# Turning the probabilities of a causal attention by VectorE block transposes and DMA in place of seven of ten TensorE transposes

## The chip, the cores and the metric

One Trainium2 chip, of which the kernel uses one core. The time is the device time of one launch in microseconds; of the kernel before it is 533.88 us, the median of 3 runs (533.76 to 533.94).

## The reference

The input is x of shape (2, 512, 256): two sequences ("halves") of 512 tokens. Four blocks are computed one after the other, each with its own parameter-free layer norm and a residual add.

```
x = x + attention0(layernorm(x))   # 3 heads, softmax over the query axis, mean over heads, fc
x = x + ffn(layernorm(x))          # ternary weights, silu(up) * gate, down
x = x + attention1(layernorm(x))   # 16 heads of 128, causal, biases
x = x + int8_linear(layernorm(x))  # per-token and per-row quantisation
```

The change is in attention1 alone. For each half b and head h it computes

```
q = x Wq + bq ; k = x Wk + bk ; v = x Wv + bv          # 512 x 128 each
scores = q k^T / sqrt(128), masked where key > query   # 512 x 512
attn   = softmax(scores over keys)
z      = attn v ;  out += z Wo ; out += bo
```

All of it is in float32. The kernel gets that accuracy from pairs of float32r operands: each operand is kept as a high part and a low part (operand minus high part), and a product is three matmuls, high*high, high*low and low*high (`split_mm`, L303 to L305).

## The kernel before, in words

Attention1 runs as 32 windows; window w is one half of the batch and one head. `PAIR_OF` and `HALF_OF` give the pair of heads and the half of each group of two windows; a pair of heads serves two groups, so its weights serve four windows. Tokens lie in four chunks of 128 (c = 0 to 3). Chunk c of the queries sees only key chunks 0 to c.

The work of one window, step by step:

- Q and K (`project_qk`, letters Q and K): two groups of six matmuls over 512 columns into PSUM; ScalarE writes the high part with the bias, VectorE the low part (`project_lo`, L1281). V (letter V, `project_v`): twelve matmuls over 256 columns, then a copy (L788) and a subtraction (L1278), letter W on ScalarE and VectorE.
- Scores (letter S, `scores`, L549 to L551): per chunk c three float32r matmuls over (c+1)*128 columns, but never under 256 (`n = max((c + 1) * P, 2 * P)`). VectorE adds the mask and takes the row maximum into `SM` (`max1`, L1291), ScalarE takes the exponential into `PR` and the row sum (`exp1`, L797), VectorE the reciprocals (`recip1`, letter R, L1298; R0 for chunks 0 to 2, R1 for chunk 3), GpSimd multiplies each chunk by them (`normalise`, L962 to L971, semaphore `p_norm`).
- The turn (letter T, `turn`, L559): to be the operand of the next product the probabilities must stand with the keys on the partitions. Chunk c takes c+1 TensorE transposes of 128 x 128 into PSUM bank 4 or 5, so a window has 1+2+3+4 = 10 of them. ScalarE copies the high part to `PT_hi` (`probs_hi`, L802), VectorE subtracts for `PT_lo` (`probs_lo`, L1302, semaphore `t_free`).
- z (letter A, or B when it belongs to the window before; `attend`): for each key chunk j three matmuls over the query columns from j*128 to 512, but never under 256. The zero blocks that the wider products read are set once. ScalarE and VectorE write `Z_hi` and `Z_lo` (L808, L1309).
- The output product (letter O, `project_out`): for both heads of a group together, 24 matmuls over 256 columns per half of the tokens, two such parts per group, then an add to X by VectorE (`add_out`, L1322).

Nothing is scheduled at run time. The order of the work on each engine is a string of letters with the chunk or part number, written by hand, one for even and one for odd windows, and the last windows have their own:

```python
EVEN_PE = steps("T0 T1 S0 O0 T2 T3 S1 Q0 S2 O1 K1 A0 S3 V2")
EVEN_DVE = steps("T0 T1 S0 W2 O0 T2 T3 S1 Q0 S2 O1 R0 K1 S3 A0 R1")
ODD_PE = steps("T0 T1 S0 Q0 T2 T3 S1 S2 K1 A0 S3 V2")
```

In window w, T and A are of window w, S and R of window w+1, Q, K and V of window w+2. Both output parts of a group fall in the even window, so even windows are longer than odd ones. Engines meet by semaphores only, and each engine works strictly in the order of its own string.

Four windows share one packed weight tile `stage` (1,027 KB, loaded by SyncE, L334). VectorE and GpSimd split it (`load_a`, `load_b`, `split_a`, `split_b`: L1214 to L1230 and L929, L935), and SyncE loads the next one when both have finished with it. In the steady windows SyncE has nothing else to do.

Of the kernel before, what the change touches and what calls it, by code (L numbers as in the profile page):

```python
# [15 lines left out]
F32 = mybir.dt.float32  # L16
# [7 lines left out]
P = 128  # L24
D = 256
# [11 lines left out]
FFN_STEPS = HALVES * ECH  # L37

# [15 lines left out]
def build(nc, x, wq0, wk0, wv0, fcT, fcb, wupT, wgateT, wdownT, pack1, bo1, qw, qb, out):  # L54
    ctx = ExitStack()
    with ctx:
# [74 lines left out]

        XQ1 = sb("XQ1", [P, CT, D])
# [16 lines left out]
        Z_hi = sb("Z_hi", [P, 2, SEQ], F32R)  # L149
        Z_lo = sb("Z_lo", [P, 2, SEQ], F32R)  # L150
# [8 lines left out]
        memf = ExitStack()  # L159
        SIL = sb("SIL", [P, 3, SEQ], F32, memf)  # L160
        HID = sb("HID", [P, 3, SEQ], F32, memf)
        HID_hi = sb("HID_hi", [P, 3, SEQ], F32R, memf)
        HID_lo = sb("HID_lo", [P, 3, SEQ], F32R, memf)
        memf.close()
# [42 lines left out]
        t_psum, pt_hi, t_free, pt_zero = sem("t_psum"), sem("pt_hi"), sem("t_free"), sem("pt_zero")  # L207
# [28 lines left out]
        LAST = {"pe": {WINDOWS - 2: steps("T0 T1 S0 S1 O0 S2 T2 T3 S3 O1"),  # L236
                       WINDOWS - 1: steps("T0 T1 B0 T2 A0 T3 O0 A1 O1 I0 I1")},
                "act": {WINDOWS - 2: steps("T0 T1 S0 S1 T2 S2 T3 W2 S3"),
                        WINDOWS - 1: steps("T0 T1 B0 T2 A0 T3 A1 X0 I0 I1")},
                "dve": {WINDOWS - 4: steps("T0 T1 S0 W2 O0 T2 T3 S1 L0 Q0 S2 O1 L1 R0 K1 S3 A0 R1 L2"),  # L240
                        WINDOWS - 3: steps("T0 T1 S0 W2 N0 Q0 T2 T3 S1 N1 S2 R0 K1 N2 S3 A0 R1 N3"),
                        WINDOWS - 2: steps("T0 T1 S0 S1 X0 S2 T2 R0 T3 W2 S3 O0 R1 X1 X2 O1"),
                        WINDOWS - 1: steps("T0 T1 B0 T2 A0 T3 X3 O0")}}

# [12 lines left out]

        def loads_k(w):

            return w % 2 == 1 and (w + 3) // 2 in FIRST_GROUP[1:]  # L260

        def window_work(engine, w):

            for kind, c in LAST[engine].get(w, ORDERS[engine][w % 2]):
                if w == 0 and kind == "O":
                    continue
                yield kind, c

# [43 lines left out]
        def _(sp):  # L312
# [33 lines left out]
        def _(pe):  # L346
# [192 lines left out]
            def scores(w, c):  # L539
# [6 lines left out]
                n = max((c + 1) * P, 2 * P)  # L546
# [7 lines left out]
            def turn(w, c):  # L554

                pe.wait_ge(p_norm, 4 * w + c + 1)
                pe.wait_ge(t_free, 4 * w + c + 1)
                for j in range(c + 1):
                    mm = pe.transpose(bank[4 + c % 2][:, j * P:(j + 1) * P], PR[:, c, j * P:(j + 1) * P], ident[:])  # L559
                mm.then_inc(t_psum, 1)  # L560

            def attend(w):

                g, h = divmod(w, 2)
                pe.wait_ge(t_free, 4 * w + 6)
# [3 lines left out]
                if w == 1:  # L569
                    pe.wait_ge(pt_zero, 1)  # L570
                for j in range(CT):
                    q0 = min(j * P, SEQ - 2 * P)
# [6 lines left out]
            def attend_half(r):  # L579
# [3 lines left out]
                pe.wait_ge(t_free, 4 * w + 4 + 2 * r)  # L583
                cols = slice(2 * r * P, 2 * (r + 1) * P)
                for j in range(2 * r + 2):
                    v = (slice(None), CT * (g % 2) + j, slice(h * DH, (h + 1) * DH))
                    mm = split_mm(pe, bank[2 + r][:, cols], V_hi[v], V_lo[v], PT_hi[w % 2][:, j, cols],
                                  PT_lo[w % 2][:, j, cols],
                                  j == 0, j == 2 * r + 1)
                mm.then_inc(z_psum, 1)  # L590

            def project_out(g, r):
# [9 lines left out]
                for i in range(2):  # L602
                    cols = slice((2 * r + i) * P, (2 * r + i + 1) * P)
                    for h in range(2):
                        mm = split_mm(pe, out_bank(g, r)[:, i * D:(i + 1) * D], Z_hi[:, h, cols], Z_lo[:, h, cols],
# [22 lines left out]
            def window(w):  # L628
                p = PAIR_OF[w // 2]
                for kind, c in window_work("pe", w):  # L630
# [13 lines left out]
                    elif kind == "O":  # L644
                        project_out(w // 2 - (w < WINDOWS - 1), c)
# [38 lines left out]
        def _(act):  # L684
# [115 lines left out]
            def probs_hi(w, c):  # L800
                act.wait_ge(t_psum, 4 * w + c + 1)
                act.copy(PT_hi[w % 2][:, 0:c + 1, c * P:(c + 1) * P],  # L802
                         bank[4 + c % 2][:, 0:(c + 1) * P].rearrange("p (j q) -> p j q", q=P)).then_inc(pt_hi, 1)

            def z_high(w):
                p, b, h = place(w)
                act.wait_ge(z_psum, w + 1)
                act.activation(Z_hi[:, h, :], bank[6][:], ACT.Identity, bias=bv[p % 2][:, h:h + 1],  # L808
                               scale=1.0).then_inc(z_hi, 1)

            def z_high_half(r):
                p, b, h = place(WINDOWS - 1)
                cols = slice(2 * r * P, 2 * (r + 1) * P)
                act.wait_ge(z_psum, WINDOWS + r)
                act.activation(Z_hi[:, h, cols], bank[2 + r][:, cols], ACT.Identity, bias=bv[p % 2][:, h:h + 1],
# [24 lines left out]

            def scale_tokens():
# [7 lines left out]
            def window(w):  # L849
                p = PAIR_OF[w // 2]  # L850
                for kind, c in window_work("act", w):
# [4 lines left out]
                    elif kind == "A" and w < WINDOWS - 1:  # L856
                        act.wait_ge(bv_ready, p + 1)
                        z_high(w)
                    elif kind == "A":
# [6 lines left out]
                    elif kind == "W":  # L866
                        if w == 0:
                            layernorm_hi(5)
                        project_hi(w + 1, c)
                    elif kind == "X":  # L870
# [14 lines left out]
        def _(pool):  # L885
# [99 lines left out]

            rstd(5)
# [17 lines left out]
        def _(dve):  # L1004
# [263 lines left out]
            dve.memset(PT_hi[0][:, CT - 1, 2 * P:3 * P].bitcast(F32), 0.0).then_inc(t_free, 1)  # L1268
            dve.memset(PT_lo[0][:, CT - 1, 2 * P:3 * P].bitcast(F32), 0.0).then_inc(t_free, 1)
# [30 lines left out]
            def probs_lo(w, c):  # L1300
                dve.wait_ge(pt_hi, 4 * w + c + 1)
# [89 lines left out]
            def window(w):  # L1391
                for kind, c in window_work("dve", w):
                    if kind == "T":
                        probs_lo(w, c)
                    elif kind == "S":
# [6 lines left out]
                    elif kind == "R":  # L1402
                        recip1(w + 1, c)
                    elif kind == "A" and w < WINDOWS - 1:
# [5 lines left out]
                    elif kind == "O":  # L1410
                        if w == 2 and c == 0:
                            dve.wait_ge(x_biased, 2 * TILES)
                        add_out(w // 2 - (w < WINDOWS - 1), c)
                    elif kind in "QK":
                        project_lo(w + 2, c)
                    elif kind == "W":
# [3 lines left out]
                        if loads_v(w):  # L1420
                            load_a(PAIR_OF[w // 2 + 1], 2)
# [9 lines left out]
                    if loads_v(w) and (kind, c) == (("O", 1) if w == WINDOWS - 8 else ("S", 1)):  # L1431
                        load_bv(PAIR_OF[w // 2 + 1])
# [68 lines left out]
```

## Time and profile before

| | |
|---|---|
| median of 3 runs | 533.88 us |
| the profiled execution | 534.24 us |
| its span | 532.4 us |
| TensorE busy | 514.5 us, 97% |
| VectorE busy | 385.2 us, 72% |
| ScalarE busy | 292.8 us, 55% |
| GpSimd busy | 191.9 us, 36% |
| chain that ended last | TensorE 86%, VectorE 7%, ScalarE 2%, DMA 2% |
| DMA | 17.52 MB in 8333 packets, most of it before 60 us |

The span is what the profiler saw between the first and the last instruction; 1.8 us of the execution lie outside it. Matmuls overlap, so a matmul's recorded time is longer than the distance to the next one; what a group of them costs is read from the distances between starts. In the tables of groups a name stands without its number, so `bank` is any PSUM bank and `PT_lo` either of the two.

### The profile page before, as it was taken

What the parts mean: (1) busy time and instruction counts of PE and PEld (TensorE: products, weight loads), DVE (VectorE), ACT (ScalarE), POOL (GpSimd) and SP (SyncE); (2) the same over time, 40 slices, a digit from 0 to 9 for tenths busy, and PEclk for the clock granted to TensorE, in tenths of its full rate; (3) what the DMA queues carried; (4) which work ended last, traced back from release to release, by engine and by line L of the source; (5) the groups of instructions that cost most, each with busy time, mean ns of one, the idle gap of its engine ahead of it and who ended that gap; (6) DMA issues with size and microseconds to landing.
All of it is one profiled execution on the core that took longest, in us unless ns stands there. A gap on an engine that the chain in (4) does not pass through costs nothing.

```text
span 532.4 us, 9326 instructions
## 1 busy us (share of the span) xinstructions
PE 514.5 (97%) x3302; PEld 464.4 (87%) x3302; DVE 385.2 (72%) x970; ACT 292.8 (55%) x688; POOL 191.9 (36%) x277
## 2 busy tenths in 40 slices
PE   8999999999999899999999999999999999999972
PEld 7888889898888789999999999999998999999861
DVE  2757876855555978768668668777777787667897
ACT  2446533564545565655656656566566565665552
POOL 2236142434656335214223223322512543222234
PEclk9999999999999999999999999999999999999995
DMA  9900000000000021000200200200200200000002
GB/s 281 356 6 1 1 0 1 2 1 1 2 0 1 0 81 46 36 1 1 80 1 1 81 2 1 79 2 2 80 0 2 80 2 0 2 1 0 2 2 79
DMA packets 8333, 17.52 MB, mean 33 GB/s; under 512 B 480, under 2 KB 6752, under 8 KB 7264
## 3 DMA queue, kind: packets, MB, share of 16 engines
q1 hardware_dynamic: 7200, 15.89, 8.7%
q10 hardware_dynamic: 1088, 1.05, 0.6%
q8 instruction: 27, 0.44, 0.3%
q14 instruction: 18, 0.15, 0.1%
HBM read 15.88 MB, written 1.05 MB: 32 GB/s over the span
## 4 chain that ended last, share of the span: by engine, by line
PE 86%; DVE 7%; ACT 2%; DMA 2%; issue 1%; POOL 1%; SPq 0%; DVEq 0%; ACTq 0%
PE bank L303 20%; PE bank L305 20%; PE bank L304 20%; PE bank L559 6%; PE bank L550 4%; PE bank L549 4%; PE bank L551 4%; PE bank L488 3%; PE bank L487 3%; DMA Wv_sb<-wv 2%; PE bank L498 1%; PE bank L500 1%; DVE XN L1021 1%; DVE SM L1291 1%; PE bank L354 1%
## 5 line engine op out<-in xcount | busy, mean ns | idle before, releaser
L797 ACT ACTIVATE PR<-SM,nmax 128x128 f32<-128x128 f32 (+3 forms) x128 | 71.9, 562 | 100.7 <-DVE nmax L1291 100.5
L1291 DVE CUSTOM_DVE_ANT_0 SM<-bank,causal 128x128 f32<-128x128 f32 (+3 forms) x128 | 60.7, 484 | 18.4 <-PE bank L551 18.3
L962 POOL TENSOR_TENSOR PR<-PR,rec 128x128 f32<-128x128 f32 x32 | 12.8, 400 | 140.2 <-DVE rec L1298 140.2
L1302 DVE TENSOR_TENSOR PT_lo<-bank,PT_hi 128x128 fp32r<-128x128 f32 (+3 forms) x128 | 59.3, 485 | 2.1 <-ACT PT_hi L802 0.3
L802 ACT CAST PT_hi<-bank 128x128 fp32r<-128x128 f32 (+3 forms) x128 | 50.0, 423 | 5.1 <-PE bank L559 4.3
L303 PE MATMUL bank<-XT_hi,W_hi 128*128 128x512 f32 x128 | 50.6, 395 | 0.2 <-DVE XT_lo L1029 0.2
L918 POOL TENSOR_TENSOR E_lo<-E,E_hi 128x512 fp32r<-128x512 f32 x24 | 31.0, 1297 | 54.6 <-ACT E_hi L721 47.6
L305 PE MATMUL bank<-XT_hi,W_lo 128*128 128x512 f32 x128 | 50.5, 395 | 0.0
L304 PE MATMUL bank<-XT_lo,W_hi 128*128 128x512 f32 x128 | 50.4, 394 | 0.0
L559 PE MATMUL bank<-ident,PR 128*128 128x128 f32 x320 | 46.2, 273 | 1.8 <-DVE PT_lo L1302 0.8
L549 PE MATMUL bank<-K_hi,Q_hi 128*128 128x256 f32 (+2 forms) x128 | 46.5, 364 | 0.0
L1281 DVE SCALAR_TENSOR_TENSOR Q_lo<-bank,bqk,Q_hi 128x512 fp32r<-128x512 f32 x32 | 24.0, 751 | 29.6 <-ACT Q_hi L791 29.6
L303 PE MATMUL bank<-PT_hi,V_hi 128*128 128x256 f32 (+2 forms) x130 | 41.9, 323 | 0.2 <-DVE V_lo L1278 0.2
L305 PE MATMUL bank<-PT_hi,V_lo 128*128 128x256 f32 (+2 forms) x130 | 41.9, 322 | 0.0
L304 PE MATMUL bank<-PT_lo,V_hi 128*128 128x256 f32 (+2 forms) x130 | 41.9, 322 | 0.0
L550 PE MATMUL bank<-K_lo,Q_hi 128*128 128x256 f32 (+2 forms) x128 | 41.5, 324 | 0.0
L559 PEld LDWEIGHTS bank<-ident,PR 128*128 128x128 f32 x320 | 37.0, 141 | 5.1 <-POOL PR L971 1.1
L551 PE MATMUL bank<-K_hi,Q_lo 128*128 128x256 f32 (+2 forms) x128 | 41.3, 322 | 0.0
L716 ACT ACTIVATE E<-bank,nmax 128x512 f32<-128x512 f32 x24 | 16.5, 687 | 41.8 <-DVE nmax L1094 41.7
L303 PE MATMUL bank<-WO_hi,Z_hi 128*128 128x256 f32 x128 | 35.8, 280 | 1.9 <-DVE Z_lo L1316 1.9
L969 POOL TENSOR_TENSOR PR<-PR,rec 128x128 f32<-128x128 f32 x32 | 13.6, 424 | 64.6 <-DVE rec L1298 64.6
L303 PE MATMUL bank<-W_hi,XT_hi 128*128 128x256 f32 x128 | 36.1, 282 | 0.0
(174 smaller groups left out, 1621.9 us busy)
## 6 DMA issues: line engine op xcount, KB each, us to landing
stage<-pack SPq DMA_DIRECT2D x8, 1027.0 KB, 4.9
X<-x SPq DMA_DIRECT2D x2, 512.0 KB, 8.8
wraw<-wupT SPq DMA_DIRECT2D x1, 1024.0 KB, 10.1
wraw<-wgateT SPq DMA_DIRECT2D x1, 1024.0 KB, 12.0
wraw<-wdownT SPq DMA_DIRECT2D x1, 1024.0 KB, 15.8
Wq_sb<-wq ACTq DMA_DIRECT2D x3, 256.0 KB, 5.3
Wk_sb<-wk SPq DMA_DIRECT2D x3, 256.0 KB, 4.7
Wv_sb<-wv SPq DMA_DIRECT2D x3, 256.0 KB, 8.4
```

Of the source, the lines that this page charges most:

```text
L303: pe.matmul(dst, a_hi, b_hi, start=first, stop=False, skip_group_check=share)
L304: pe.matmul(dst, a_hi, b_lo, start=False, stop=False, skip_group_check=share)
L305: return pe.matmul(dst, a_lo, b_hi, start=False, stop=last, skip_group_check=share)
L549: pe.matmul(dst[:, 0:n], Q_hi[:, slot, cols], K_hi[:, slot, 0:n], start=True, stop=False)
L550: pe.matmul(dst[:, 0:n], Q_hi[:, slot, cols], K_lo[:, slot, 0:n], start=False, stop=False)
L551: pe.matmul(dst[:, 0:n], Q_lo[:, slot, cols], K_hi[:, slot, 0:n], start=False, stop=True).then_inc(s_psum, 1)
L559: mm = pe.transpose(bank[4 + c % 2][:, j * P:(j + 1) * P], PR[:, c, j * P:(j + 1) * P], ident[:])
L797: act.activation(PR[:, c, 0:(c + 1) * P], SM[:, c % 2, 0:(c + 1) * P], ACT.Exp, bias=nmax1[:, c:c + 1], scale=-1.0, accum_out=sum1[:, c:c ...
L802: act.copy(PT_hi[w % 2][:, 0:c + 1, c * P:(c + 1) * P], bank[4 + c % 2][:, 0:(c + 1) * P].rearrange("p (j q) -> p j q", q=P)).then_inc(pt_ ...
L918: pool.tensor_tensor(E0_lo[:, m, :], E0[:, m, :], E0_hi[:, m, :], ALU.subtract).then_inc(e0_lo, 1)
L1291: dve.tensor_tensor_reduce(SM[:, c % 2, 0:n], bank[2 + c % 2][:, 0:n], causal[:, SEQ - n:SEQ], 1.0, HIGHEST, ALU.add, ALU.min, nmax1[:, c: ...
L1302: dve.tensor_tensor(PT_lo[w % 2][:, 0:c + 1, c * P:(c + 1) * P], bank[4 + c % 2][:, 0:(c + 1) * P].rearrange("p (j q) -> p j q", q=P), PT_ ...
```

## The change

For windows 1 to 25 (`FIRST_MOVED` to `LAST_MOVED`) chunks 2 and 3 are no longer turned by TensorE. In their place:

- VectorE transposes 32 x 32 blocks in place of the grid (`turn_blocks`, letter U; U2 at the end of the window before, U3 early in its own window) from `PR` into `BT`, 384 and 512 columns.
- SyncE then issues 16 DMAs per window from `BT` to `MV`, one for each pair (i, j) of 32-partition groups. Each moves 32 partitions x 8 runs of 32 floats, which is 32 KB in 256 runs of 128 bytes. Diagonal groups (i = j) are moved in the same way. `BT` and `MV` are double-buffered.
- One window later ScalarE copies `MV` to `PT_hi` (`moved_hi`, letter C) and GpSimd subtracts for `PT_lo` (`moved_low`, semaphore `mv_lo`). VectorE's two subtractions for these chunks go. The product z of window w comes in window w+1 (letter B) and waits for `mv_lo`.

With it go these edits: the output product has one part in every window instead of two in every other one, `Z_hi` and `Z_lo` are double-buffered for it; the weight tile is loaded from ScalarE's queue (`refill`, behind W2 of a window) instead of SyncE's; scores of chunk 0 and z of key chunk 3 run over 128 columns instead of 256 in all windows, and the zero blocks that the wider products needed are no longer written; `BT`'s one block that no transpose writes is set to zero by GpSimd; SIL, HID and their parts lie at other addresses. Windows 26 to 31 turn all chunks on TensorE as before; window 26 computes two z products.

```diff
-        ODD_DVE = steps("T0 T1 S0 W2 Q0 T2 T3 S1 S2 R0 K1 S3 A0 R1")
-        ORDERS = {"pe": (EVEN_PE, ODD_PE), "act": (EVEN_ACT, ODD_ACT), "dve": (EVEN_DVE, ODD_DVE)}
...
+        FIRST_MOVED, LAST_MOVED = 1, WINDOWS - 7
+        STEADY_PE = (steps("T0 T1 S0 O0 S1 Q0 S2 K1 S3 B0 V2"), steps("T0 T1 S0 Q0 S1 O0 S2 K1 S3 B0 V2"))
+        STEADY_ACT = (steps("W2 T0 T1 S0 C2 C3 S1 Q0 S2 K1 B0 S3"),
+                      steps("W2 T0 T1 S0 Q0 C2 C3 S1 S2 K1 B0 S3"))
+        STEADY_DVE = (steps("S0 W2 U3 T0 T1 O0 S1 Q0 S2 R0 K1 S3 B0 R1 U2"),
+                      steps("S0 W2 U3 T0 T1 S1 Q0 O0 S2 R0 K1 S3 B0 R1 U2"))
...
@@ sync
-            for p in range(1, PAIRS):
-
-                sp.wait_ge(wb_dve, p)
-                sp.wait_ge(wb_pool, p)
-                sp.dma_start(stage[:], pack1[p]).then_inc(ld_pack, 16)
+            sp.wait_ge(bt_zero, 1)
+            for w in range(FIRST_MOVED, LAST_MOVED + 1):
+                sp.wait_ge(bt_done, 2 * moved_windows(w + 1))
+                if w >= FIRST_MOVED + 2:
+                    sp.wait_ge(mv_lo, 2 * moved_windows(w - 1))
+                for j in range(CT):
+                    for i in range(CT):
+                        sp.dma_start(MV[w % 2][j * QUAD:(j + 1) * QUAD, :, :, i * QUAD:(i + 1) * QUAD],
+                                     BT[w % 2][i * QUAD:(i + 1) * QUAD, :, :, j * QUAD:(j + 1) * QUAD]
+                                     ).then_inc(moved[w % 2], 16)
...
@@ scores
-                n = max((c + 1) * P, 2 * P)
+                n = (c + 1) * P
...
@@ attend
-                pe.wait_ge(t_free, 4 * w + 6)
+                pe.wait_ge(t_free, turns(w + 1))
+                if by_dma(w):
+                    pe.wait_ge(mv_lo, 2 * moved_windows(w + 1))
...
-                    q0 = min(j * P, SEQ - 2 * P)
+                    q0 = j * P
...
@@ scalar
+            def moved_hi(w, c):
+                if c == 2:
+                    act.wait_ge(moved[w % 2], MOVES * ((w - FIRST_MOVED) // 2 + 1))
+                act.copy(PT_hi[w % 2][:, 0:c + 1, c * P:(c + 1) * P], MV[w % 2][:, 0:c + 1, c - 2, :]).then_inc(mv_hi, 1)
...
+            def refill(p):
+
+                act.wait_ge(wb_dve, p)
+                act.wait_ge(wb_pool, p)
+                act.dma_start(stage[:], pack1[p]).then_inc(ld_pack, 16)
...
@@ gpsimd
+            def moved_low(w):
+
+                for c in range(2, CT):
+                    pool.wait_ge(mv_hi, 2 * moved_windows(w) + c - 1)
+                    pool.tensor_tensor(PT_lo[w % 2][:, 0:c + 1, c * P:(c + 1) * P], MV[w % 2][:, 0:c + 1, c - 2, :],
+                                       PT_hi[w % 2][:, 0:c + 1, c * P:(c + 1) * P], ALU.subtract).then_inc(mv_lo, 1)
...
             def window(w):
 
+                if by_dma(w - 1):
+                    moved_low(w - 1)
...
@@ vector
+            def turn_blocks(w, c):
+                dve.wait_ge(p_norm, 4 * w + c + 1)
+                if c == 2:
+                    dve.wait_ge(bt_zero, 1)
+                    if w >= FIRST_MOVED + 2:
+                        dve.wait_ge(moved[w % 2], MOVES * ((w - FIRST_MOVED) // 2))
+                dve.transpose(BT[w % 2][:, 0:c + 1, c - 2, :],
+                              PR[:, c, 0:(c + 1) * P].rearrange("p (j q) -> p j q", q=P)).then_inc(bt_done, 1)
```

## Rows read from the trace of the kernel before

**Rows 1.** The page: busy time of engines, then the chain that ended last.
```profile
PE 514.5 (97%) x3302; PEld 464.4 (87%) x3302; DVE 385.2 (72%) x970; ACT 292.8 (55%) x688; POOL 191.9 (36%) x277
...
PE 86%; DVE 7%; ACT 2%; DMA 2%; issue 1%; POOL 1%; SPq 0%; DVEq 0%; ACTq 0%
```

**Rows 2.** Busy time by stretch: from:to, length, busy us (count) of each engine.
```profile
203.20:487.00 283.80, 283.80 (x1884) 261.70 (x1883) 213.66 (x568) 171.32 (x429) 91.45 (x156) 1.00 0.07 23
```

**Rows 3.** Timeline of TensorE: start, length, first matmuls of three windows in turn.
```profile
341.49 0.49 PE L559 MATMUL bank<-ident,PR 128*128 128x128 f32 x3
...
350.67 0.49 PE L559 MATMUL bank<-ident,PR 128*128 128x128 f32 x3
...
362.58 0.49 PE L559 MATMUL bank<-ident,PR 128*128 128x128 f32 x3
```

**Rows 4.** Timeline of TensorE around one turn of chunks 2 and 3.
```profile
331.41 0.28 PE L304 MATMUL bank<-WO_lo,Z_hi 128*128 128x256 f32 x1
331.52 0.28 PE L305 MATMUL bank<-WO_hi,Z_lo 128*128 128x256 f32 x1
331.64 0.93 PE L559 MATMUL bank<-ident,PR 128*128 128x128 f32 x7
332.32 0.36 PE L549 MATMUL bank<-K_hi,Q_hi 128*128 128x256 f32 x1
332.52 0.28 PE L550 MATMUL bank<-K_lo,Q_hi 128*128 128x256 f32 x1
```

**Rows 5.** Timeline of TensorE: plain float32 matmuls over 128 and over 256 columns.
```profile
82.45 0.60 PE L387 MATMUL bank<-diag,ones 128*128 128x128 f32 x4
...
5.11 5.65 PE L380 MATMUL bank<-Wk_sb,Wq_sb 128*128 128x256 f32 x24 [0.35 <-DMA Wk_sb<-wk]
```

**Rows 6.** Groups by shape, 200 to 480 us: xcount | busy us, mean ns | idle before.
```profile
L1302 DVE TENSOR_TENSOR PT_lo<-bank,PT_hi 128x512 fp32r<-128x512 f32 x26 | 17.7, 683 | 0.0
L1302 DVE TENSOR_TENSOR PT_lo<-bank,PT_hi 128x384 fp32r<-128x384 f32 x26 | 14.3, 549 | 0.9
...
L1222 DVE CAST W_hi<-stage 128x512 fp32r<-128x512 f32 x7 | 5.8, 830 | 0.0
...
L1219 DVE CAST W_hi<-stage 128x512 fp32r<-128x512 f32 x7 | 2.8, 406 | 0.0
...
L802 ACT CAST PT_hi<-bank 128x512 fp32r<-128x512 f32 x26 | 15.5, 595 | 0.0
...
L802 ACT CAST PT_hi<-bank 128x384 fp32r<-128x384 f32 x27 | 12.8, 476 | 4.4 <-PE bank L559 3.6
...
L929 POOL TENSOR_TENSOR W_lo<-stage,W_hi 128x512 fp32r<-128x512 f32 x14 | 18.1, 1295 | 2.5 <-DVE W_hi L1222 2.5
```

**Rows 7.** Timelines of VectorE, ScalarE and GpSimd behind the window start at 341.49.
```profile
341.95 0.16 DVE L1298 RECIPROCAL rec<-sum 128x1 f32<-128x1 f32 x1 [0.22 <-ACT PR L797]
...
342.97 0.69 DVE L1278 TENSOR_TENSOR V_lo<-bank,V_hi 128x512 fp32r<-128x512 f32 x1
...
343.39 0.19 ACT L797 ACTIVATION_READ_ACCUMULATOR PR<-SM,nmax 128x1 f32 x1
...
342.58 0.59 POOL L971 TENSOR_SCALAR PR<-PR,rec 128x384 f32<-128x384 f32 x1
```

**Rows 8.** Timeline of TensorE: first matmul of z, of S3 and of V, same pair.
```profile
337.43 0.39 PE L303 MATMUL bank<-PT_hi,V_hi 128*128 128x512 f32 x1
...
339.37 0.40 PE L549 MATMUL bank<-K_hi,Q_hi 128*128 128x512 f32 x1
...
340.07 0.28 PE L303 MATMUL bank<-W_hi,XT_hi 128*128 128x256 f32 x1
```

**Rows 9.** SyncE's DMA issues (ns min/median/max of one); then its timeline while queues are full.
```profile
L334 SPq DMA_DIRECT2D stage<-pack x7: 327/328/340, 189.7 to 421.2; - x7
...
L340 SPq DMA_DIRECT2D out<-OUT x3: 372/394/398, 526.9 to 529.9; - x3
...
DMA to landing us min/median/max: 2.1/2.3/3.0
...
9.67 0.67 SPq L325 DMA_DIRECT2D wraw<-wupT  x1
10.38 0.67 SPq L325 DMA_DIRECT2D wraw<-wgateT  x1
```

**Rows 10.** The page: DMA queues (packets, MB, share of 16 engines' span); one kind of issue.
```profile
q10 hardware_dynamic: 1088, 1.05, 0.6%
...
stage<-pack SPq DMA_DIRECT2D x8, 1027.0 KB, 4.9
```

**Rows 11.** Busy time by stretch with one weight load in it; last: DMA share, GB/s.
```profile
250.00:260.00 10.00, 10.00 (x68) 9.15 (x68) 6.58 (x20) 6.09 (x16) 3.68 (x6) 1.00 0.30 107
```

More of the change, by code:

```diff
@@ L37 @@
 FFN_STEPS = HALVES * ECH
+QUAD = P // 4
+MOVES = 16 * 16
 H1 = 16
@@ L130, in build @@
         memt.close()
+        memb = ExitStack()
+        BT = [sb(f"BT{i}", [P, CT, 2, P], F32, memb) for i in range(2)]
+        MV = [sb(f"MV{i}", [P, CT, 2, P], F32, memb) for i in range(2)]
+        memb.close()
         XQ1 = sb("XQ1", [P, CT, D])
@@ L206, in build @@
         s_psum, s_max, s_exp, s_rec, p_norm = (sem(n) for n in ("s_psum", "s_max", "s_exp", "s_rec", "p_norm"))
-        t_psum, pt_hi, t_free, pt_zero = sem("t_psum"), sem("pt_hi"), sem("t_free"), sem("pt_zero")
+        t_psum, pt_hi, t_free = sem("t_psum"), sem("pt_hi"), sem("t_free")
+        bt_zero, bt_done = sem("bt_zero"), sem("bt_done")
+        moved = [sem(f"moved{i}") for i in range(2)]
+        mv_hi, mv_lo = sem("mv_hi"), sem("mv_lo")
         z_psum, z_hi, z_free = sem("z_psum"), sem("z_hi"), sem("z_free")
@@ L256, in loads_v, with loads_o, by_dma, moved_windows @@
             return w % 2 == 0 and w // 2 + 1 in FIRST_GROUP[1:]
+        def loads_o(w):
+            return PAIRS - 1 if w == WINDOWS - 6 else PAIR_OF[w // 2 + 1] if loads_v(w) and w < WINDOWS - 8 else 0
         def loads_k(w):
             return w % 2 == 1 and (w + 3) // 2 in FIRST_GROUP[1:]
+        def by_dma(w):
+            return FIRST_MOVED <= w <= LAST_MOVED
+        def moved_windows(w):
+            return max(0, min(w, LAST_MOVED + 1) - FIRST_MOVED)
+        def turns(w):
+            return CT * w - 2 * moved_windows(w)
+        def out_part(w, c):
+            if w > LAST_MOVED + 2:
+                return w // 2 - (w < WINDOWS - 1), c
+            if w == LAST_MOVED + 2:
+                return w // 2 - 1, c
+            return (w - 3) // 2 if w % 2 else (w - 4) // 2, 1 - w % 2
         def window_work(engine, w):
-            for kind, c in LAST[engine].get(w, ORDERS[engine][w % 2]):
-                if w == 0 and kind == "O":
+            for kind, c in ORDERS[engine][w]:
+                if w <= 2 and kind == "O":
                     continue
                 yield kind, c
+        def stage_refill(w):
+            return 1 if w == 0 else PAIR_OF[w // 2 + 1] + 1 if loads_v(w) and w < WINDOWS - 8 else 0
         LN_BANKS = {0: (0, 1), 1: (0, 1), 2: (0, 1), 3: (0, 1), 4: (0, 1), 5: (6, 7)}
@@ L858, in window @@
                         z_high(w)
+                    elif kind == "C":
+                        moved_hi(w - 1, c)
                     elif kind == "A":
@@ L869, in window @@
                         project_hi(w + 1, c)
+                        if w > 0 and stage_refill(w - 1):
+                            refill(stage_refill(w - 1))
                     elif kind == "X":
@@ L984, in window @@
                     split_a(PAIR_OF[(w + 3) // 2], 1)
+            pool.wait_ge(down_done, FFN_STEPS)
+            for turned in BT:
+                last = pool.memset(turned[:, CT - 1, 0, :], 0.0)
+            last.then_inc(bt_zero, 1)
             rstd(5)
@@ L1394, in window @@
                         probs_lo(w, c)
+                        if c == 1 and loads_v(w):
+                            load_a(PAIR_OF[w // 2 + 1], 2)
                     elif kind == "S":
@@ L1403, in window @@
                         recip1(w + 1, c)
+                    elif kind == "U":
+                        turn_blocks(w + 1 if c == 2 else w, c)
+                        if c == 3 and loads_k(w - 1):
+                            load_a(PAIR_OF[(w + 2) // 2], 1)
                     elif kind == "A" and w < WINDOWS - 1:
```

110 lines of the change are left out of this document (62 added, 48 removed).

## The prediction

> **What bounds the kernel now.** I read the page first. TensorE is busy 97% of the span and carries 86% of the chain that ended last; no other engine has over 72% and 7% [rows 1]. Next the long stretch of steady windows: over 283.8 us TensorE is busy for all of it, at the full granted clock of 1.00, VectorE for 213.66 us, ScalarE for 171.32, GpSimd for 91.45, and the DMA engines for 7% [rows 2]. So in attention1 time goes only if TensorE work goes. Then the period: the odd window takes 350.67 - 341.49 = 9.18 us, the even one behind it 11.91, a window 10.55 us on the average [rows 3]. The stretch of 283.8 us is 26.9 such windows, so per window VectorE works 213.66 / 26.9 = 7.94 us, ScalarE 6.37 and GpSimd 3.40.
>
> **What goes on TensorE.** Seven transposes per window. Around them the last matmul before starts at 331.52 and the second one after at 332.52 [rows 4], a distance of 1.00 us. The matmuls before stand 0.11 to 0.12 apart, so two of them without the transposes would take 0.23. The seven cost 1.00 - 0.23 = 0.77 us. In 25 windows that is 19.3 us, all of it on the path.
>
> **Narrow matmuls.** Six float32r matmuls per window (three for S0, three for key chunk 3 of z) go from 256 to 128 columns. The trace has no float32r matmul over 128 columns. At 256 columns one takes 0.115 [rows 4]. Lower end: half, 0.058, which gives 6 x 0.057 = 0.34 us per window, 11 us over the 32 windows. Upper end: the plain float32 records over 128 columns come in 0.11 ((0.60 - 0.27) / 3) [rows 5], and a plain float32 matmul has two records (this line's loop issues two matmuls and four records are there), 0.22 in all (over 256 columns a record takes 0.23, so the price follows the columns, same group); that would cost 6 x 0.105 = 0.63 us per window, 20 us in 32 windows. Nearest are rows with a single record, 128 columns and their own weight load: the transposes, 0.68 / 7 = 0.097 [rows 4]. From 0.115 to 0.097 is 6 x 0.018 = 0.1 us per window, 3 us in all, and since plain float32 stands on the other side I count zero.
>
> **VectorE.** Two subtractions of 549 and 683 ns go, two block transposes of 384 and 512 columns come. No block transpose is in the trace. Copies of 512 columns from SBUF to SBUF take 406 and 830 ns in two places [rows 6]; these are my bounds, and I take 0.47 and 0.60, near the mean and near the subtractions. Per window 7.94 - 1.23 + 1.07 = 7.8 us, or at the upper bound 7.94 - 1.23 + 1.45 = 8.2, under the new period of 9.78. It is not free all the same: the three windows in four that split weights have up to 1.3 us more on VectorE, ahead of what ScalarE and GpSimd wait for, with less room to catch up in than before. I allow 0.4 us in each of six windows, 2.4 us. Both ends: 0, and 0.4 in every one of the 25, 10 us.
>
> **ScalarE and GpSimd.** Two copies of 476 and 595 ns are replaced by two of the same shapes from SBUF, one window later [rows 6]: zero, between -0.2 and +0.3 us per window by the spread of the two SBUF casts in the same rows, hidden behind TensorE since ScalarE is busy 6.4 of 9.78 us. One DMA issue of about 0.33 us [rows 9] comes to it in seven windows. GpSimd gets 1.295 us for 512 columns and, in proportion, 0.97 for 384: 3.40 + 2.27 = 5.7 us per window, hidden. The waits on the two finished weight halves in front of that issue are met one window earlier. Double buffers, later addresses and the spread of the output product over both windows cost nothing: TensorE has the same matmuls, only one part of 2.7 us per window pair moves.
>
> **The moves.** This is the term that decides. Each DMA has 256 runs of 128 bytes, so 16 packets on each of 16 DMA engines plus one for the semaphore. What does one cost?
> On the issue side: SyncE takes 0.33 us for the 128 runs of a weight load, 0.37 to 0.40 for the stores of 256 and 512 runs of 1 KB, and 0.67 when the queues are full, with 0.04 between two [rows 9]. I take 0.39 + 0.04 = 0.43 us; ends 0.37 and 0.71. Sixteen take 6.9 us (5.9 to 11.4).
> On the engine side: ScalarE's queue moved 1 KB packets; 0.6% of 16 x 532.4 us is 51 us for 1088 packets, 47 ns each [rows 10]. If only bytes counted, 128 bytes would take 6 ns; if only packets, 47. Per DMA that is 17 x 6 = 0.1 us or 17 x 47 = 0.80 us, per window 1.6 or 12.8 us. The trace has no small data packet. I take 25 ns, about the middle, 0.43 us per DMA, the issue rate.
>
> Is this in time? Clock 0 is the first turn of window w (341.49 now). The reciprocal of chunk 3 comes at 0.46, GpSimd has it applied at 1.68, V_lo ends at 2.17 [rows 7]. U3 stands behind V_lo, so it ends at 2.8 and SyncE starts. The last of 16 is issued at 2.8 + 6.9 = 9.7 and lands some 1.9 us later (2.3 from the start of an issue), at 11.6, which is 1.8 into the next window. There ScalarE comes to C2 after the exponential of S0, at 343.58, so 2.1, in even windows and after Q0, about 3.0, in odd ones: no wait. From C2 on: 0.48, then 0.97 and 1.3 on GpSimd, so `mv_lo` is complete at 4.9 (even) or 5.8 (odd). TensorE wants it at the z product. The z product takes 1.94 us and V 1.42 [rows 8, 3], so it starts at 9.78 - 3.36 = 6.4. Slack: 1.5 or 0.6 us. Behind the waiting `attend` on TensorE stands everything; behind the waiting C2 on ScalarE stand the exponentials S1 to S3 of the next window, so lateness over about 1.5 us is paid by the path in full.
>
> **Weight loads against moves.** Seven loads are now issued at about 1.2 in windows 1, 3, 7, ... 23 and occupy all DMA engines for 0.30 x 10 = 3.0 us [rows 11], landing after 4.9 [rows 10]. They overlap the first moves. With 16 x 0.43 = 6.9 us of packets in the queue the moves end up to 2 us later, over the slack by some 0.5. I charge 0.3 us x 7 = 2 us; ends 0 and 2 us x 7 = 14 us.
>
> **Edges.** Windows 1 and 2 fill the pipeline, window 26 has two z products and a turn before Q0: 2 us, ends 0 and 5.
>
> **Sum** against the profiled execution: 534.24 - 19.3 + 0 + 2.4 + 2 + 2 = 521.3 us. The runs' median is 0.36 below it: 521.
>
> **A rule of the Trainium skill.** No row shows what a small packet costs. The page "DMA: Bandwidth & Descriptors", Specifications, puts the least transfer for line rate at 512 bytes and says that below it the engine reads, modifies and writes; at 128 bytes that speaks against this change, for rival 1. The same page, "Why small descriptors are slow", exempts transfers within SBUF and names 128-byte packets at 78% of a link's rate; by that the packets would be hidden. The page "VectorE: DVE Perf Modes", "The three transpose paths", has a block transpose of 128 x 128 bf16 at 311 ns; as an estimate, three and four of them make 0.93 and 1.24 us, VectorE would stand at 8.9 us per window and rival 4 would hold.
>
> **Rivals.**
> 1. The packets bound the window (slower). If a packet takes 47 ns like a 1 KB one, 16 DMAs take 12.8 us and, since SyncE's queue then never runs dry, so does a window: 25 x (12.8 - 10.55) = 56 us more, 590 us. By the timing above the window grows beyond 10.55 from about 0.6 us per DMA, 35 ns per packet. For it: 128-byte runs, both sides scattered. Against it: 47 ns for 1 KB is 22 bytes per ns, so a large part of it is bytes. Chance 0.25; its range 540 to 600.
> 2. SyncE's issue bounds. If an issue takes the 0.67 + 0.04 us of full queues, 16 take 11.4 us: 25 x 0.8 = 20 us more, 554. Against it: those queues held megabytes. With late landings of a milder kind 0.15, 530 to 556.
> 3. Narrow matmuls at two records (slower): 521 + 20 = 541, or down to 532 where TensorE would have stalled anyway. For it: plain float32 pays it. Against it: the transposes of 128 columns, with a weight load each, come in 0.097 [rows 4]. 0.10.
> 4. VectorE paces: transposes at the upper bound or dearer, everything behind U3 and U2 later; 0.4 us in each window instead of six, 529. 0.08.
> 5. The forecast as summed, own range 514 to 529. 0.42.
>
> **Numbers.** What a measurement of this kernel can tell from no change is 0.2%, 1.1 us. Faster: 0.42, 0.06 of rival 4, 0.02 each of rivals 2 and 3: 0.52. Same: 0.02 each of rivals 2 and 3, 0.01 of rival 4: 0.05. Slower: 0.25, 0.11 of rival 2, 0.06 of rival 3, 0.01 of rival 4: 0.43. Range 514 to 592: below it are narrow matmuls at half the time, above it packets dearer than 1 KB ones.
>
> **What would show it.** Window starts 9.6 to 9.9 us apart and alike for even and odd ones confirm the TensorE term. The idle time of TensorE at the first matmul of z, released by GpSimd's `PT_lo`, and of ScalarE at the copy from `MV`, released by DMA, are zero or small if the moves are in time; several us per window show rival 1 or 2. Which: the issues of SyncE at 0.4 us with a DMA share near 1 say packets, issues at 0.7 with a low share say issue. Distances of the S0 matmuls tell rival 3, the length of the transposes rival 4. I am wrong if the windows are over 10.5 us apart.

## The result, and the profile after

The changed kernel takes 575.89 us, the median of 4 runs (572.27 to 579.01), against 533.91 us for the kernel before (533.76 to 534.23): a ratio of 1.078, 95% interval 1.072 to 1.085. It is slower by 42 us. The forecast was 521 us, the range 514 to 592; the sign was wrong, and the time that came lies in the range only by rival 1 (packets, 540 to 600), whose mechanism did not happen; rival 2, the nearest to what did, ended at 556. Where two executions of one kernel lie over 1.5% apart, the faster one is compared.

The page of the changed kernel, in parts: busy times, the clock that was granted in 40 slices, DMA, queues, chain.

```profile
PE 512.4 (90%) x3127; PEld 454.2 (80%) x3127; DVE 387.5 (68%) x968; ACT 290.8 (51%) x688; POOL 248.8 (44%) x325
...
PEclk9999999999999988899899799989999989999996
...
q1 hardware_dynamic: 114992, 21.66, 19.5%
...
PE 71%; DVE 11%; issue 9%; ACT 4%; SPq 2%; DMA 1%; POOL 1%; DVEq 0%; ACTq 0%
```

TensorE has fallen from 97% to 90% of a longer span and from 86% to 71% of the chain [rows 1]. The granted clock, 9 tenths or more in all steady slices before, now shows 7 and 8 among them.

Who waited for whom in the changed kernel (total us, times, longest):

```profile
POOL PT_lo L1060 <- ACT PT_hi L878: 78.9, 24, 6.1
...
ACT PT_hi L878 <- DMA MV<-BT: 57.7, 20, 4.4
...
PE bank L367 <- issue: 35.7, 18, 3.7
```

This is one chain read backwards: TensorE stands at the z product (the `issue` waits are those at `attend`, which waits for `mv_lo`), GpSimd stands for ScalarE's copy, and ScalarE's copy stands for the moves. The kernel before had no such wait.

TensorE's timeline, first transposes of four windows in turn, and the z product inside each (the end of a row: idle time before it):

```profile
327.90 0.49 PE L629 MATMUL bank<-ident,PR 128*128 128x128 f32 x3
...
337.67 0.49 PE L629 MATMUL bank<-ident,PR 128*128 128x128 f32 x3
...
345.95 0.47 PE L367 MATMUL bank<-PT_hi,V_hi 128*128 128x512 f32 x1 [1.69 <-issue]
...
349.37 0.49 PE L629 MATMUL bank<-ident,PR 128*128 128x128 f32 x3
...
356.74 0.47 PE L367 MATMUL bank<-PT_hi,V_hi 128*128 128x512 f32 x1 [0.76 <-issue]
...
360.14 0.49 PE L629 MATMUL bank<-ident,PR 128*128 128x128 f32 x3
...
370.22 0.47 PE L367 MATMUL bank<-PT_hi,V_hi 128*128 128x512 f32 x1 [3.51 <-issue]
...
375.18 0.49 PE L629 MATMUL bank<-ident,PR 128*128 128x128 f32 x3
```

The first window takes 9.77 us: nothing waits, and this is the period that the transposes' removal promised (10.55 on the average before, [rows 3]). The next three take 11.70, 10.77 and 15.04. The pattern repeats every four windows, which is the rhythm of the weight loads.

SyncE's issues in the changed kernel (count: ns min/median/max), and how long a move takes to land:

```profile
L401 SPq DMA_DIRECT2D MV<-BT x400: 585/611/1806, 196.7 to 492.5; - x134
...
DMA to landing us min/median/max: 1.9/2.0/5.8
```

An issue is 0.61 us where the prediction counted 0.39 [rows 9]. With 0.04 between two, 16 take 10.4 us, and the window without waits has 9.77. The mean issue is longer still, 0.64 us: 22 of the 400 took over 0.8 us, up to 1.8. These belong to windows without a weight load as well as with one, and the longest comes at 441.1 us with the next load at 453.7; what they are stays open. By the mean, 16 take 10.9 us.

The latest landings do belong to the weight loads. Window 10 issues its moves from 303.9 to 314.7 us, and ScalarE issues the load of 1 MB at 312.12, when the next window has begun (311.86). The eleven moves before it, the five with or behind it, and ScalarE's copy that waits for the last of them:

```profile
L401 SPq DMA_DIRECT2D MV<-BT x11: 586/611/1661, 303.9 to 311.5; - x11
...
DMA to landing us min/median/max: 1.9/2.0/3.1
...
312.12 0.33 ACTq L922 DMA_DIRECT2D stage<-pack  x1
...
L401 SPq DMA_DIRECT2D MV<-BT x5: 610/611/613, 312.1 to 314.7; - x5
...
DMA to landing us min/median/max: 4.5/5.1/5.8
...
319.28 1.03 ACT L878 CAST PT_hi<-MV 128x384 fp32r<-128x384 f32 x2 [4.41 <-DMA MV<-BT]
```

In windows 2, 6, 14, 18 and 22 it is the same with the last three or four moves. The prediction let a load meet the first moves of a window, which have time. It meets the last ones of the window before, because their issue reaches 1.8 to 2.9 us into the next window.

The packets themselves are cheap: the kernel without the moves (below) has 6192 packets and 4.8% on this queue, so 108,800 packets took 0.195 x 16 x 570.5 - 0.048 x 16 x 520.6 = 1,380 us of engine time, 12.7 ns each (6,400 of them are the semaphores' own).

What a long wait does to the clock, by stretches of the changed kernel (busy us and count of PE, PEld, DVE, ACT, POOL, then the granted clock, DMA share, GB/s):

```profile
309.00:318.50 9.50, 9.46 (x62) 8.40 (x60) 7.05 (x21) 4.88 (x12) 4.19 (x7) 1.00 0.70 161
318.50:322.10 3.60, 0.00 (x0) 0.00 (x0) 0.26 (x2) 2.70 (x7) 2.23 (x3) 0.77 0.32 46
322.10:328.00 5.90, 5.81 (x25) 5.55 (x26) 2.57 (x6) 1.39 (x3) 1.72 (x4) 0.56 0.31 47
```

TensorE idles for 3.7 us at z in a window with a load. The clock falls within that wait (mean 0.77), and behind it the mean granted clock is 0.56, which is the lower of its two levels, 1.2 GHz, for most of 5.9 us. The four windows above make 47.28 us, against 39.39 for four in the kernel without moves. Of the 7.9 us more, 5.96 are the waits in the rows. The other 1.9 fit the lower clock: behind the wait that ends at 370.22 its mean is 0.66 over 4.96 us, and 0.34 x 4.96 = 1.7.

### The profile page after: what moved, and what is told of

Same layout as the page of the kernel before. It is cut to its first block, busy times and chain, and to the rows that moved or that the text cites. A ratio compares the mean times of both kernels' runs of the same rounds, so it can differ in the third digit from the quotient of the medians.

```text
span 570.5 us, 9406 instructions
## 1 busy us (share of the span) xinstructions
PE 512.4 (90%) x3127; PEld 454.2 (80%) x3127; DVE 387.5 (68%) x968; ACT 290.8 (51%) x688; POOL 248.8 (44%) x325
## 4 chain that ended last, share of the span: by engine, by line
PE 71%; DVE 11%; issue 9%; ACT 4%; SPq 2%; DMA 1%; POOL 1%; DVEq 0%; ACTq 0%
PE bank L367 18%; PE bank L369 17%; PE bank L368 17%; PE bank L619 3%; PE bank L620 3%; PE bank L556 3%; PE bank L557 3%; PE bank L618 3%; DVE SM L1385 2%; PE bank L629 2%; SPq L401 2%; ACT PR L867 2%; DVE XN L1117 2%; PE bank L567 1%; PE bank L569 1%
## 5 line engine op out<-in xcount | busy, mean ns | idle before, releaser
L1060 POOL TENSOR_TENSOR PT_lo<-MV,PT_hi 128x384 fp32r<-128x384 f32 (+1 forms) x50 | 59.5, 1210 | 78.9 <-ACT PT_hi L878 78.9
L367 PE MATMUL bank<-PT_hi,V_hi 128*128 128x128 f32 (+3 forms) x130 | 43.8, 337 | 37.8 <-issue 35.7
L367 PEld LDWEIGHTS bank<-PT_hi,V_hi 128*128 128x128 f32 x130 | 26.3, 202 | 48.4 <-issue 44.3
L878 ACT CAST PT_hi<-MV 128x384 fp32r<-128x384 f32 (+1 forms) x50 | 25.8, 562 | 57.7 <-DMA MV<-BT 57.7
L369 PE MATMUL bank<-PT_hi,V_lo 128*128 128x128 f32 (+3 forms) x130 | 44.4, 342 | 0.0
L368 PE MATMUL bank<-PT_lo,V_hi 128*128 128x128 f32 (+3 forms) x130 | 44.2, 340 | 0.0
L1413 DVE SCALAR_TENSOR_TENSOR Z_lo<-bank,bv,Z_hi 128x512 fp32r<-128x512 f32 x31 | 23.2, 749 | 29.7 <-ACT Z_hi L884 29.5
L618 PE MATMUL bank<-K_hi,Q_hi 128*128 128x128 f32 (+3 forms) x128 | 43.2, 337 | 0.0
L619 PE MATMUL bank<-K_lo,Q_hi 128*128 128x128 f32 (+3 forms) x128 | 41.5, 324 | 0.0
L620 PE MATMUL bank<-K_hi,Q_lo 128*128 128x128 f32 (+3 forms) x128 | 41.4, 324 | 0.0
```

The source lines that it names most:

```text
L367: pe.matmul(dst, a_hi, b_hi, start=first, stop=False, skip_group_check=share)
L368: pe.matmul(dst, a_hi, b_lo, start=False, stop=False, skip_group_check=share)
L369: return pe.matmul(dst, a_lo, b_hi, start=False, stop=last, skip_group_check=share)
L618: pe.matmul(dst[:, 0:n], Q_hi[:, slot, cols], K_hi[:, slot, 0:n], start=True, stop=False)
L619: pe.matmul(dst[:, 0:n], Q_hi[:, slot, cols], K_lo[:, slot, 0:n], start=False, stop=False)
L620: pe.matmul(dst[:, 0:n], Q_lo[:, slot, cols], K_hi[:, slot, 0:n], start=False, stop=True).then_inc(s_psum, 1)
```

## The experiments

Theory I: SyncE's issue costs a fixed 0.65 us whatever the DMA holds, and 16 of them do not fit. Theory P: the issue is held up by the packets behind it.

### The change without its moves

```diff
-                for j in range(CT):
-                    for i in range(CT):
-                        sp.dma_start(MV..., BT...)
...
-                act.copy(PT_hi[w % 2][...], MV[w % 2][...])
+                act.copy(PT_hi[w % 2][...], BT[w % 2][...])
```

> The changed kernel without its 400 DMAs: ScalarE and GpSimd read BT where they read MV, and VectorE waits for the reader of BT instead of for the moves, so the quarters of each block stay where they are and are not exchanged. All else as changed. If the moves alone cost what was lost, TensorE does not wait at z, windows are 9.7 to 9.9 us apart also where weights are loaded, the granted clock stays at 1.00, and the time is 518 to 525 us. If the rest of the rebuild (orders, narrow matmuls, block transposes, GpSimd's subtractions) costs as well, it is 530 us or more.

Measured: 521.97 us (521.16 to 522.5, 4 runs), ratio 0.977, interval 0.975 to 0.979. No wait of TensorE at z over 0.1 us. A stretch of four windows, one with a load in it:

```profile
254.21:293.60 39.39, 39.29 (x255) 35.59 (x253) 32.67 (x86) 25.26 (x64) 22.86 (x32) 1.00 0.08 28
```

That is 9.85 us per window at a granted clock of 1.00. The prediction's sum without its 2 us for loads beside moves is 519, so all of it but the moves was right to 3 us, and the moves with what they collide with cost 54 us.

### Half the runs, the same number of DMAs

```diff
-    MV[w % 2][j * QUAD:(j + 1) * QUAD, :, :, i * QUAD:(i + 1) * QUAD]
+    MV[w % 2][j * QUAD:(j + 1) * QUAD, 0:2, :, i * QUAD:(i + 1) * QUAD]
...
```

> The changed kernel with the same 16 DMAs per window, each of half the runs (4 of 8 per partition; the other half of MV is set to zero once and not moved). Theory I, an issue of SyncE costs a fixed time: an issue stays at 0.6 us and the time within 8 us of the changed kernel's 572 to 579. Theory P, the issue takes as long as the packets or descriptors behind it: an issue falls to 0.30 to 0.40 us, TensorE no longer waits at z in windows without a weight load, and the time falls under 550 us.

Measured: 559.03 us (a second execution took 568.05), issues of 585/601/1537 ns. The issue did not follow the runs, as theory I has it. But against 572 to 579 us some 13 to 20 came back: more than the 8 that theory I allowed, less than theory P wanted. The waits at z in the six windows with a load fell from 3.3 to 3.7 us to 2.7 to 3.1, and those in the ten late windows between them from 13.3 to 9.2 us in sum. So packets do count, by about 4 us in each kind of window; the rest is not taken apart.

### Eight DMAs of twice the width

```diff
-                for j in range(CT):
+                for j in range(2):
...
-    MV[w % 2][j * QUAD:(j + 1) * QUAD, :, :, i * QUAD:(i + 1) * QUAD]
+    MV[w % 2][j * 2 * QUAD:(j + 1) * 2 * QUAD, :, :, i * QUAD:(i + 1) * QUAD]
...
-    BT[w % 2][i * QUAD:(i + 1) * QUAD, :, :, j * QUAD:(j + 1) * QUAD]
+    BT[w % 2][i % 2 * 2 * QUAD:(i % 2 + 1) * 2 * QUAD, :, :, j * QUAD:(j + 1) * QUAD]
```

> The changed kernel with 8 DMAs per window of 64 partitions instead of 16 of 32: the same bytes and the same number of runs of 128 bytes, wrong places. Theory I: an issue stays near 0.6 us, the moves of a window take 8 x 0.65 = 5.2 us, the time falls to 520 to 540 us. Theory P: an issue grows to about 1.2 us and the time stays at 565 to 580.

Measured: 522.87 us (two runs), ratio 0.979, interval 0.977 to 0.981. The same bytes in the same 128-byte runs, and the loss is gone. Its queue and issues:

```profile
q1 hardware_dynamic: 111792, 21.64, 21.5%
...
L401 SPq DMA_DIRECT2D MV<-BT x200: 590/635/1892, 197.6 to 440.5; - x100
...
DMA to landing us min/median/max: 2.0/2.3/4.1
```

Twice the runs per DMA, 0.635 us instead of 0.611. This decides between I and P: it is the count of DMAs.

### One dimension less in the pattern

```diff
-    MV[w % 2][j * QUAD:(j + 1) * QUAD, :, :, i * QUAD:(i + 1) * QUAD]
+    MV[w % 2][j * QUAD:(j + 1) * QUAD].rearrange("p k t q -> p (k t) q")[:, :, i * QUAD:(i + 1) * QUAD]
...
```

> The changed kernel with the key block and the chunk of each DMA written as one dimension of 8 in place of 4 x 2; same result, same DMAs. If the number of dimensions of the pattern makes the issue dear, an issue falls from 0.61 towards 0.4 us and the time under 550; if it does not (theories I and P in any other form), nothing moves: 0.6 us and 570 to 580.

Measured: 573.97 us (569.83 and 578.12), issues 585/611/1601 ns. Nothing moved.

### Weight loads cut short

```diff
-                act.dma_start(stage[:], pack1[p]).then_inc(ld_pack, 16)
+                act.dma_start(stage[:, 0:64], pack1[p][:, 0:64]).then_inc(ld_pack, 16)
```

> The changed kernel with the seven weight loads beside the moves cut from 2,054 columns to 64 (most of the weights of later pairs are then those of pair 0; same work otherwise). Theory I now says: 16 issues of 0.65 us alone keep TensorE waiting for 0.8 to 1.7 us in two of four windows; the loads add the waits of 3.3 to 3.7 us and the stretches at half clock behind them. Expected: no wait over 2 us, granted clock 1.00 in the steady stretch, windows of 10.5 to 11 us and 540 to 552 us in all. If the loads are innocent it stays at 572 to 579; if they are the whole loss it falls to 525 or less.

Measured: 554.46 us (553.29 and 555.62), ratio 1.037, interval 1.034 to 1.040; just above what was expected. The longest wait at z is 2.1 us, and the steady windows are 9.7 to 12.1 us with three of 13.4 to 13.7. That is where the expectation missed: the granted clock still fell to its lower level behind waits of 1.9, 1.8 and 2.1 us. The loads thus account for 575.9 - 554.5 = 21 us and the issues alone for 554.5 - 522.0 = 32 us. Rival 2 of the prediction, 16 x 0.71 = 11.4 us a window, had 554; the windows here average 11.1, part of it by the clock.

What the loads cost is mostly waiting. TensorE's waits at `attend` were 35.7 us in the changed kernel, and are here:

```profile
PE bank L367 <- issue: 22.0, 20, 2.1
```

The two profiled spans are 570.5 and 553.8 us, 16.7 apart, and 13.7 of that are these waits.

### Narrow matmuls alone

```diff
-                n = max((c + 1) * P, 2 * P)
+                n = (c + 1) * P
...
-                    q0 = min(j * P, SEQ - 2 * P)
+                    q0 = j * P
```

> The kernel before with one part of the change alone: scores of chunk 0 and z of key chunk 3 over 128 columns instead of 256 (in the last window z stays at 256). Forecast of the prediction: no effect, 533 to 535 us, distance of two such matmuls 0.11 to 0.12 us. Rivals: half the time per matmul, 523 us; two records as in plain float32, 550 us or more.

Measured: 533.44 us (10 runs) against 534.43 for the kernel before beside it, ratio 0.998, interval 0.997 to 0.999. In the changed kernel the three scores of chunk 0 and what follows stand 0.11 to 0.14 apart:

```profile
312.10 0.31 PE L618 MATMUL bank<-K_hi,Q_hi 128*128 128x128 f32 x1
...
312.24 0.27 PE L619 MATMUL bank<-K_lo,Q_hi 128*128 128x128 f32 x1
312.35 0.28 PE L620 MATMUL bank<-K_hi,Q_lo 128*128 128x128 f32 x1
312.47 0.45 PE L367 MATMUL bank<-XT_hi,W_hi 128*128 128x512 f32 x1
```

A float32r matmul of 128 columns takes about what one of 256 does, 0.115 [rows 4]. The zero in the sum was right to 1 us.

### What makes an issue dear

> The kernel without the 400 moves, and on SyncE's idle queue 28 DMAs into memory that nothing reads, four of each of seven forms: 32 partitions x 8 runs of 128 bytes between SBUF tiles (the change's form), 32 partitions x 1 KB, 128 partitions x 8 runs of 128 bytes, 128 partitions x 1 KB, and from HBM 32 partitions x 1 KB, 128 partitions x 1 KB, 32 partitions x 8 runs. Which of them makes the issue 0.6 us: if it is the runs, forms 1, 3 and 7 take 0.6 and the others 0.35; if it is SBUF as a source, forms 1 to 4 take 0.6 and 5 to 7 0.35 to 0.4; if it is 32 partitions instead of 128, forms 1, 2, 5 and 7 do. The time stays at 522.

Measured: 522.56 us in one run, and for the seven forms (ns min/median/max of four issues each):

```profile
L397 SPq DMA_DIRECT2D MV<-MV x4: 604/610/744, 175.5 to 177.6; - x4
...
L401 SPq DMA_DIRECT2D MV<-MV x4: 564/590/592, 179.6 to 181.4; - x4
...
L404 SPq DMA_DIRECT2D MV<-MV x4: 679/688/690, 183.3 to 185.5; - x4
...
L407 SPq DMA_DIRECT2D MV<-MV x4: 488/601/943, 188.8 to 190.9; - x4
...
L410 SPq DMA_DIRECT2D MV<-pack x4: 352/420/423, 193.0 to 194.4; - x4
...
L413 SPq DMA_DIRECT2D MV<-pack x4: 353/579/877, 197.2 to 199.0; - x4
...
L416 SPq DMA_DIRECT2D MV<-pack x4: 343/450/453, 201.9 to 203.3; - x4
```

The order is that of the expectation. With 32 partitions, SBUF to SBUF costs 0.61 in eight runs per partition (L397) and 0.59 in one (L401); HBM to SBUF costs 0.42 in one run (L410) and 0.45 in eight (L416). So at up to 256 runs a transfer with both ends in SBUF costs 0.16 to 0.17 us more to issue than one from HBM. SBUF as a source is not enough for that: a write from SBUF to HBM takes 0.33 (next section). L413 scatters too widely to say.

Runs cost little, but not nothing. Between SBUF tiles the medians are 0.590 for 32 runs (L401), 0.601 for 128 (half the runs), 0.611 for 256, 0.635 for 512 (eight wide) and 0.688 for 1,024 (L404, 128 partitions), about 0.1 ns for each run. At 1,024 runs the difference between the ends is not seen either: the reads from HBM in the next section, with a pattern of another form, take 0.684.

A queue's state counts too. In the groups from HBM the least time, 0.34 to 0.35, is that of the first of the four, and the later ones take 0.42 or more. The stores and weight loads from which the prediction took its price have one end in HBM and were issued one at a time [rows 9]; both lowered it.

### The exchange through HBM

```diff
+                sp.dma_start(scratch[w % 2], BT[w % 2][:].rearrange("p k t q -> p (k t q)")).then_inc(parked[w % 2], 16)
...
+                sp.wait_ge(parked[w % 2], 16 * ((w - FIRST_MOVED) // 2 + 1))
                 for j in range(CT):
-                    for i in range(CT):
-                        sp.dma_start(MV..., BT...)
+                    sp.dma_start(MV[w % 2][j * QUAD:(j + 1) * QUAD].rearrange("a k t (i b) -> a (k t) i b", b=QUAD),
+                                 scratch[w % 2].rearrange("(i a) (k q) -> a k i q", a=QUAD, q=P)
+                                 [:, :, :, j * QUAD:(j + 1) * QUAD]).then_inc(moved[w % 2], 16)
```

> Meant to be better than both: the same exchange of blocks with 5 DMAs per window instead of 16. One writes BT to a scratch in HBM (128 rows of 4 KB), SyncE waits for it, and four read it back, one for each group of 32 partitions of MV, 1,024 runs of 128 bytes each. Same result. Theory I: 5 issues of 0.4 to 0.7 us, landing of the write 2.2 us and of the reads 2.5 to 3.5 us: complete 8 to 9 us after the transposes, no wait at z, windows of 9.8 us and 520 to 526 us. If small packets from HBM are dear (47 ns each as for 1 KB), a window's reads take 12 us and the time is 590.

Measured: 524.52 us (523.51 to 525.17, 4 runs), ratio 0.981, interval 0.979 to 0.983. It computes the same result and beats both kernels, the one before by 10 us. TensorE waits at z three times in the steady part, 0.4 to 0.7 us each. Its two kinds of issue:

```profile
L399 SPq DMA_DIRECT2D scratch<-BT x25: 325/326/343, 198.1 to 437.2; - x25
...
L404 SPq DMA_DIRECT2D MV<-scratch x100: 557/684/1817, 202.6 to 441.9; - x100
...
scratch<-BT SPq DMA_DIRECT2D x25, 512.0 KB, 2.6
MV<-scratch SPq DMA_DIRECT2D x100, 128.0 KB, 3.8
```

By medians 0.33 + 4 x 0.68 = 3.1 us of issues replace 16 x 0.61 = 9.8. In `scratch` the row of a block is split and permuted within one DMA (`(i a) (k q) -> a k i q`), so one read gathers from all four source groups; whether a pattern on an SBUF source could do this was not tried. The rival of the expectation, dear small packets from HBM, did not happen: the 128-byte packets took 13 ns each in this trace.

### Twelve moves, and moves from two queues

```diff
+                        if i == j:
+                            continue
```

> The changed kernel with 12 DMAs per window: the four diagonal groups are left out (their places in MV are zero) and nothing else takes over. Theory I: 12 x 0.65 = 7.8 us of issues, moves complete 2.8 + 7.8 + 1.9 = 12.5 us after the window's start, in time where no weight load is beside them; with a load TensorE waits at z for up to 1 us. 523 to 530 us. If the loads cost by themselves whatever the number of moves, the waits of 2 us and more stay in every fourth window and the time is over 540.

Measured: 526.26 us (523.55 and 528.97), ratio 0.985, interval 0.973 to 0.997. Waits at z only with a load, 0.2 to 0.7 us, once 2.3 at the start. The place of the threshold is theory I's: 12 x 0.65 = 7.8 us fit and 16 do not, while 16 DMAs with half the packets stayed at 559. The wait of 2.3 us is in the one window whose last move (214.2 us) was issued next to the load (214.4) and took 5.9 us to land; in the other windows the moves are issued before the load, or 2.5 us and more behind it, and land in 2.7 us at most.

```diff
+                        if kind == "K" and by_dma(w):
...
+                                act.dma_start(MV[w % 2][q, :, :, q], BT[w % 2][q, :, :, q]).then_inc(moved[w % 2], 16)
```

> The changed kernel with the four diagonal moves issued from ScalarE's queue behind the high part of K, the other 12 by SyncE; same 16 DMAs, same result. If the 0.6 us per issue belong to the queue that issues, the two run side by side and the time is near that of the kernel with 12 moves, plus what 4 x 0.6 us cost ScalarE: 524 to 534 us, SyncE's issues stay at 0.61. If one generator serves both queues, an issue is longer where both issue, and the time is 545 us or more.

Measured: 536.85 us (533.75 to 538.77, 4 runs), ratio 1.005, interval 0.999 to 1.011: between the 534 and the 545 us expected. SyncE's issues stay at 585/611/1920 ns while ScalarE's are 592/636/1839, so the two queues do not slow each other by the medians. What is left I put down to ScalarE's own time, which no run separates: 4 x 0.64 = 2.5 us in front of its other work, and its high part of z waits 30.6 us in all behind `issue`.

## Why the prediction was wrong

- **TensorE, 19.3 us.** Right. Windows that nothing delays are 9.77 us apart, forecast 9.78. In the kernel without moves 23 steady windows average 9.86 us, the weight splitting included.
- **Narrow matmuls, zero.** Right to 1 us (533.4 against 534.4).
- **VectorE, 2.4 us.** Right in sum. The block transposes took 0.58 and 0.70 us, for 0.47 and 0.60 assumed and 0.93 and 1.24 by the estimate quoted beside it. In the kernel without moves the windows with weight splitting are 0.1 to 0.5 us longer. Four windows take 39.39 us for 4 x 9.77 = 39.08, so about 2 us in all. Rival 4 did not come.
- **ScalarE, GpSimd.** Hidden, as said, GpSimd's subtractions with means of 1.04 and 1.38 us for 0.97 and 1.3.
- **Edges, 2 us.** By difference about 5, the upper end: the kernel without moves gains 12 us where 19.3 - 2 would be 17. Its 522 us lie close to the forecast of 521 by luck, since 521 holds 2 us for loads beside moves that it does not have.
- **Packets.** Assumed 25 ns, measured 12.7. Rival 1, the likeliest of the slower ones, did not happen. Of the two statements of the Trainium skill weighed there, both from the page "DMA: Bandwidth & Descriptors", the trace is nearer to "Why small descriptors are slow", which exempts transfers within SBUF. It does not bear that out in full: 12.7 ns is twice the 6 ns that bytes alone would give.
- **The issue: this is the step that failed.** It was priced at 0.39 + 0.04 us from transfers with one end in HBM; between SBUF tiles it is 0.61 + 0.04. With the measured price in its place and nothing else altered, the prediction's own timing gives the profile: 2.8 + 15 x 0.65 + 2.0 = 14.6 us for the last landing, 4.8 into the next window; 2.75 more for copy and subtractions is 7.5, and z was due at 6.4: a wait of 1.1 us, where the rows show 0.76 and 1.69. By the mean issue of 0.64 the last landing is 0.5 us later still, and SyncE starts each window with part of the last one's moves to issue. The prediction had the upper end, 0.71, in its bounds and this mechanism as rival 2, at a chance of 0.15, but with a range that ended at 556. A single assumed middle decided the sign, with a slack of 0.6 to 1.5 us that a surcharge of 0.04 to 0.09 us per issue uses up.
- **Weight loads, 2 us: the second term that failed.** They cost 21 us, beyond the upper end of 14. It follows from the first: 16 issues reach into the next window, so the load that ScalarE issues there meets the last three to five moves, which land after 4.4 to 5.8 us instead of 2.0. The prediction had it meet the first moves. The wait of 3.3 to 3.7 us mostly brought the lower clock on top, a cost that the prediction did not name at all. Beside moves that are in time (eight wide, twelve, through HBM) the wait at z with the same loads is under 1 us, but for the one of 2.3.

What stays open is why an issue between SBUF tiles is dearer than one with an end in HBM, what the single issues of 0.8 to 1.9 us are, and what the 3 us of the loads' price are that are not waits at z.

## What to carry to other kernels

Count DMAs before bytes: when a queue must issue n of them in each period of a loop, n times the issue time of that very kind (both ends, the number of runs, one behind another, measured) has to stay well under the period, and a price taken from another kind can be wrong by half. Once a lag exceeds what hides it, other things come on top: here the last transfers came to lie behind a large load, and long waits were followed by a lower clock of TensorE. Ask what else will be in the queues when the last transfer of a period is issued. And an exchange between partition groups that takes 16 DMAs within SBUF takes 5 through HBM.

## What the runs showed of the hardware

- An issue by SyncE: 0.33 us for SBUF to HBM with 4 KB rows. From HBM to 32 partitions 0.42 to 0.45 for 32 and 256 runs (0.34 to 0.35 for the first of a group), 0.68 for 1,024 runs. Between SBUF tiles 0.59 for 32 runs, 0.61 for 256, 0.69 for 1,024.
- Moves of 32 KB landed 2.0 us after their issue, and 4.4 to 5.8 us when a load of 1 MB was issued just before them from ScalarE.
- 128-byte packets between SBUF tiles take 12.7 ns of a DMA engine each, where 1 KB packets from HBM took 47 [rows 10].
- TensorE's granted clock had a mean of 0.56 over 5.9 us after it had idled for 3.7 us, and fell behind three waits of 1.8 to 2.1 us in the run with short loads.
- VectorE's block transpose of float32 takes 579 ns for 384 columns and 702 ns for 512.
